# Stacked q and k of three attentions, read back per group of four heads in 8 KB runs

## What is computed

```python
x = x + attn_a(layernorm(x))    # 16 q heads, 4 kv heads of 16 channels, RoPE, causal by blocks of 128
x = x + moe(layernorm(x))       # 64 experts
x = x + attn_b(layernorm(x))    # 16 q heads, 4 kv heads, window of 128 and 4 sink tokens
x = x + moe(layernorm(x))
x = x + attn_c(layernorm(x))    # 16 q heads, 16 kv heads, RoPE, all tokens seen
x = x + ffn(layernorm(x))
x = x + latent_attn(layernorm(x))
x = x + ffn(layernorm(x))

# each of a, b, c, per head (d = 16):
scores = q @ k.T / 4            # 1024 x 1024, masked
y = softmax(scores) @ v
```

## Time and profile before

| | us |
|---|---|
| median of three runs | 2221.38 |
| profiled execution, its own time | 2218.32 |
| its span | 2216.3 |
| TensorE busy | 1916.7 (86%) |
| VectorE busy | 1164.1 (53%) |
| ScalarE busy | 912.3 (41%) |
| GpSimd busy | 597.5 (27%) |
| mean granted TensorE clock | 0.911 |

### The profile page before, as it was taken

How to read it: one execution, slowest core, us unless ns; L and a number is a source line. 1 busy time by engine, 2 the same in 40 slices (tenths; PEclk the granted TensorE clock), 3 DMA queues, 4 the chain that set the end, 5 groups by cost and what they waited for, 6 DMA issues and landing times. The chain is left out here.

```text
span 2216.3 us, 30788 instructions
## 1 busy us (share of the span) xinstructions
PE 1916.7 (86%) x10273; PEld 1241.9 (56%) x10273; DVE 1164.1 (53%) x2032; ACT 912.3 (41%) x1932; POOL 597.5 (27%) x488
## 2 busy tenths in 40 slices
PE   4499689999998498699999985499976899999997
PEld 3133467888885265587888863033344455555566
DVE  4476334444444354344444456488833467777743
ACT  1177433333333265333333332087751045555531
POOL 1000246656662100456656534000000011111100
PEclk8599789999999699799999997599997599999998
DMA  2700153444430700444444401900004000000000
GB/s 75 107 1 1 38 131 102 112 123 106 106 85 0 108 2 24 97 123 115 106 103 106 126 3 51 135 8 1 1 1 102 0 1 1 0 0 0 0 1 20
DMA packets 128262, 123.11 MB, mean 56 GB/s; under 512 B 81448, under 2 KB 108208, under 8 KB 128016
## 3 DMA queue, kind: packets, MB, share of 16 engines
q1 hardware_dynamic: 128176, 121.99, 24.5%
HBM read 113.30 MB, written 8.65 MB: 55 GB/s over the span
## 5 line engine op out<-in xcount | busy, mean ns | idle before, releaser
L667 DVE TENSOR_TENSOR e_inner_lo<-e_inner_b,e_inner_hi 128x512 fp32r<-128x512 f32 x192 | 251.5, 1310 | 391.6 <-ACT e_inner_hi L614 391.6
L647 POOL TENSOR_TENSOR e_wsilu<-e_silu_b,e_rw 128x512 f32<-128x512 f32 x192 | 262.0, 1365 | 212.0 <-ACT e_silu_b L621 158.6
L554 PE MATMUL psum<-e_x_hi,e_w_hi 128*128 128x512 f32 x768 | 305.6, 398 | 5.8 <-DVE e_inner_b L678 4.4
L554 PE MATMUL psum<-e_x_lo,e_w_hi 128*128 128x512 f32 x768 | 301.1, 392 | 0.0
L554 PE MATMUL psum<-e_x_hi,e_w_lo 128*128 128x512 f32 x768 | 301.0, 392 | 0.0
L621 ACT ACTIVATE e_silu_b<-psum 128x512 f32<-128x512 f32 x192 | 114.7, 597 | 365.2 <-PE psum L554 365.2
L655 POOL TENSOR_TENSOR e_w_lo<-e_w_raw,e_w_hi 128x384 fp32r<-128x384 f32 x180 | 215.4, 1197 | 134.2 <-ACT e_w_hi L608 112.8
L1202 DVE TENSOR_REDUCE c_mx<-psum 128x1 f32<-128x1024 f32 x128 | 151.4, 1220 | 63.4 <-PE psum L1079 63.4
L554 PEld LDWEIGHTS psum<-e_x_hi,e_w_hi 128*128 128x128 f32 x768 | 145.6, 190 | 48.3 <-DVE e_inner_b L678 18.3
L1650 ACT ACTIVATE la_probs<-psum,la_negmax 128x256 f32<-128x256 f32 (+7 forms) x128 | 96.2, 752 | 175.9 <-DVE la_negmax L1737 175.9
L554 PEld LDWEIGHTS psum<-e_x_hi,e_w_lo 128*128 128x128 f32 x768 | 145.5, 189 | 31.0
(11 more groups left out here) (303 smaller groups left out, 3116.9 us busy)
## 6 DMA issues: line engine op xcount, KB each, us to landing
e_rw<-e_rw_dram SPq DMA_DIRECT2D x64, 384.0 KB, 5.8
e_rw<-e_rw_dram SPq DMA_DIRECT2D x64, 256.0 KB, 5.4
e_w_raw<-in_L_ffn_w_gate SPq DMA_DIRECT2D x64, 192.0 KB, 2.6
e_w_raw<-in_L_ffn_w_up SPq DMA_DIRECT2D x64, 192.0 KB, 2.6
e_w_raw<-in_L_ffn_w_down SPq DMA_DIRECT2D x32, 384.0 KB, 3.5
e_rw<-e_rw_dram SPq DMA_DIRECT2D x64, 128.0 KB, 5.3
a_qs<-a_parts_dram SPq DMA_DIRECT2D x12, 256.0 KB, 9.3
b_qs<-b_parts_dram SPq DMA_DIRECT2D x12, 256.0 KB, 9.4
```

The lines of the kernel that those rows point to most:

```text
L554: last = nc.tensor.matmul(bank[u % 2][:], parts.up_or_gate(a, s, which, k, j), parts.x[b][:, k, h * HALF:(h + 1) * HALF], start=(n == 0), ...
L647: nc.gpsimd.tensor_tensor(wsilu[:, u % 2, :], silu[:, u % 2, :], rw[:, s, j, h * HALF:(h + 1) * HALF], ALU.mult).then_inc(weighted, 1)
L667: nc.vector.tensor_tensor(inner_parts[1][:, u % 3, :], inner[:, u % 2, :], inner_parts[0][:, u % 3, :], ALU.subtract).then_inc(low_made, 1)
```

## The change

Three things differ. First, the parts in DRAM are laid out as (chunk, part, channel, head, token), so that four heads of one channel are 8 KB in one piece. A unit's parts are stored by three DMAs, one per part, in place of one. Second, the reads: per group of four heads, q is read in three pieces of 48, 32 and 16 partitions, each repeating one part 3, 2 or 1 times (`broadcast_to`); k, where the group has keys of its own, in three pieces that take the parts in turn. `PAIRS` is put in the order that this needs. Third, one semaphore per group: TensorE waits for a group's stacks ahead of the first maximum of phases 0, 2, 4 and 6.

```diff
-PAIRS = [(0, 0), (0, 1), (1, 0), (0, 2), (1, 1), (2, 0)]
+PAIRS = [(0, 0), (0, 1), (0, 2), (1, 0), (1, 1), (2, 0)]
...
-        stacked = [core.sem(f"{tag}_stk{c}") for c in range(HEADS * HD // P)]
+        stacked = [core.sem(f"{tag}_stk{g}") for g in range(HEADS // QUART)]
...
+RUNS = [(0, 3), (3, 2), (5, 1)]
+
+
+def stacks_of_group(cfg, g):
+
+    return len(RUNS) * (2 if cfg.kv_heads == HEADS or g == 0 else 1)
...
-    parts_dram = nc.dram_tensor(f"{tag}_parts_dram", (PARTS, C, P, T), BF16, kind="Internal").ap()
+    parts_dram = nc.dram_tensor(f"{tag}_parts_dram", (C, PARTS, HD, P // HD, T), BF16, kind="Internal").ap()
...
-                sp.dma_start(parts_dram[:, j, 0:rows_of[j], h * HALF:(h + 1) * HALF].rearrange("a p t -> p a t"),
-                             part[0:rows_of[j], :, j, h * HALF:(h + 1) * HALF]).then_inc(parts_stored, 16)
+                for w in range(PARTS):
+                    sp.dma_start(parts_dram[j, w, :, 0:rows_of[j] // HD, h * HALF:(h + 1) * HALF].rearrange("d h t -> h d t"),
+                                 part[0:rows_of[j], w, j, h * HALF:(h + 1) * HALF]).then_inc(parts_stored, 16)
...
-                sp.wait_ge(parts_stored, 16 * (n + 1))
-                for g, (pq, pk) in enumerate(PAIRS):
-                    todo = [(qs, pq, c)]
-                    if c < cfg.k_chunks:
-                        todo.append((ks, pk, QC + c))
-                    for dst, which, i in todo:
-                        heads = rows_of[i] // HD
-                        h0 = 8 * c
-                        sp.dma_start(dst[g * HD:(g + 1) * HD, h0:h0 + heads, :],
-                                     parts_dram[which, i, 0:rows_of[i], :].rearrange("(h d) t -> d h t", d=HD)
-                                     ).then_inc(stacked[c], 16)
-
+                sp.wait_ge(parts_stored, 16 * PARTS * (n + 1))
+                for g in range(2 * c, 2 * c + 2):
+                    h0 = QUART * (g % 2)
+                    todo = [(qs, c, QUART * g, h0, QUART, False)]
+                    if cfg.kv_heads == HEADS or g == 0:
+                        todo.append((ks, QC + c, QUART * g, h0, QUART, True))
+                    for dst, i, to, frm, heads, in_turn in todo:
+                        for n0, (r0, reps) in enumerate(RUNS):
+                            rows = parts_dram[i, :, :, frm:frm + heads, :].rearrange("w d h t -> w d (h t)")
+                            if in_turn:
+                                some = rows[0:reps].rearrange("w d n -> (w d) n")
+                            else:
+                                some = rows[n0:n0 + 1].broadcast_to([reps, HD, heads * T])
+                            sp.dma_start(dst[r0 * HD:(r0 + reps) * HD, to:to + heads, :].rearrange("p h t -> p (h t)"), some).then_inc(stacked[g], 16)
...
-            pe.wait_ge(stacked[0], 16 * stacks_of_chunk(cfg, 0))
             for what, *args in order:
                 if what == "max":
-                    if args == [PHASES // 2, 0, 0]:
-                        pe.wait_ge(stacked[1], 16 * stacks_of_chunk(cfg, 1))
+                    if args[0] % 2 == 0 and args[1:] == [0, 0]:
+                        pe.wait_ge(stacked[args[0] // 2], 16 * stacks_of_group(cfg, args[0] // 2))
                     maxima(*args)
```

More of the change, by code:

```diff
@@ L763, in attention @@
         project_out(core, tag, ctxs, wo, wo_loaded, extra=core.xn if tag == "c" else None)
-def stacks_of_chunk(cfg, c):
-    return len(PAIRS) * (2 if c < cfg.k_chunks else 1)
+RUNS = [(0, 3), (3, 2), (5, 1)]
+def stacks_of_group(cfg, g):
+    return len(RUNS) * (2 if cfg.kv_heads == HEADS or g == 0 else 1)
 def project_and_stack(core, tag, cfg, norm, v, qs, ks, part, wo, stacked, wo_loaded):
```

## The result

| | before | after |
|---|---|---|
| median, us | 2221.16 (20 runs) | 2226.03 (20 runs) |
| profiled execution, its own time | 2218.32 | 2225.67 |
| its span | 2216.3 | 2223.6 |

A forecast was written before the change was run, and what follows sets the result against it. DMA transfers ahead of each attention's first maximum, 72.5 us in all, were taken as the bound. Stores +20.8, reads of group 0 -16.1 and added waits nothing gave +4.7 on 2218.3: 2223, as a median 2226; range 2190 to 2243.

The forecast's parts named there:

- Stores: First store issue to stores landed, in all three attentions: 8 or 4 engines make this +20.8 us (+7.6 to +34.0).
- term of 12.6 us for the four units: Stores in a: the four units ahead of the first reads take 12.6 us from first bytes at 55.7, landing at 68.7.
- Reads of group 0: First read issue to first maximum, in all three attentions: 18.8 us each (14.6 to 21.5), sum -16.1 (-28.8 to -8.0).
- 39 rows of 0.34 us are 13.3 us: Reads of group 0: engine 0 carries most, 33 rows of q and 6 of k, 8 KB each, in 13.3 us.
- Rates by partitions: Stores and reads: rate goes by partitions touched at a time, not bytes; 337 to 386 GB/s from 128, 185 from 64.
- Few engines for a short outermost dimension: New stores and q reads: only as many of the 16 engines work as the outermost dimension (8, 4, 3, 2) has entries.
- All engines, 2181 us: First rival, stores and reads: all 16 engines carry every piece, stores cost as before, about -40 us, 2181; chance 0.15.
- The added waits: TensorE's waits ahead of phases 2, 4 and 6 cost nothing; the tightest is b, with phase 2 due 21.6 us after first maximum.
- What would show it: Signs in the trace: stores about 14 us, reads about 19 in all three, high rate 3 us, then two or three engines.

The follow-up runs named there:

- e4: The kernel before with only the new DRAM layout and three stores a unit, its own twelve reads per chunk and two semaphores kept: 2233.90 us, ratio 1.0054.
- e5: The kernel before with three stores a unit, one per part, in place of one, its own layout and reads kept: 2223.68 us, ratio 1.0012.
- e8: The changed kernel with k pieces issued ahead of q pieces and the 48-row q piece cut into 32 and 16 rows: 2220.61 us, 0.9997 of the kernel before.
- e12: The changed kernel with group 1's reads, and all behind them, issued only when group 0 has landed: 2216.44 us, 0.9974 of the kernel before.
- e3: The changed kernel with the 48-row q piece cut into 32 and 16 rows: 2224.34 us, 1.0011 of the kernel before.
- e7: The changed kernel with a group's k pieces issued ahead of its q pieces, same DMAs: 2221.01 us, 1.0001 of the kernel before.
- e1: The changed kernel with a channel's repeats next to each other, so every read's outermost dimension is 16, stores untouched: 2193.84 us, 0.9880 of the kernel before.
- e6: e2 with k's reads of the first chunk issued on ScalarE's queue in another order of blocks: 2186.32 us, 0.9840 of the kernel before.
- e10: e2, one queue, with a group's twelve pieces ordered so that neighbours write different partitions and share no block: 2189.97 us, 0.9841 of the kernel before.
- e11: e9 with group 1's reads moved from the projection's block to the attention's: 2188.36 us, 0.9837 of the kernel before.
- e2: The kernel before with only its reads and waits made per group of four heads, own stores, layout and 2 KB runs: 2192.52 us, ratio 0.9877.
- e9: The kernel before with group semaphores, one-head reads into 48, 32 and 16 partitions, channels outermost, first chunk's k on ScalarE's queue: 2194.94 us, ratio 0.9872.

## Why the prediction was right, and where it was not

The total was right: +4.7 foretold, +4.9 between the medians, +7.3 in the profiled span. The mechanism was right too: few engines, in the stores and in the reads. The sizes of its two large terms were not, and that the total came out is in good part luck.

- **Stores**, taken as +20.8 (7.6 to 34.0), were +12.3. The mechanism (8 or 4 engines) is shown by the share of 0.51 and 0.27; that the stores alone cost this, by e4. Its term of 12.6 us for the four units was an estimate that let other engines slow each one for half of the time, and no run shows it: they ran at 21 to 23 GB/s each, and 11.0, 11.2 and 11.0 us less 0.9 ahead and 0.4 behind leave 9.7 to 9.9. Nor does one show the 17.0 us that its upper end comes from, 192 rows of 1 KB at 11.6 GB/s an engine: 11.6 was measured on 64 partitions with all 16 engines. What I had at nothing, three issues a unit in place of one, is 1.9, 1.7 and 0.3 us where all engines work (e5).
- **Reads of group 0**, taken as -16.1 (-28.8 to -8.0), were -4.4, outside their own bounds. The failed step is "39 rows of 0.34 us are 13.3 us", to which I added 1 us as all that the other transfers cost. It has the engines that carry q's rows nearly alone on the memory from the start. In fact the others don't wait for them: the share is 0.95 (167 GB/s from 69 to 75 us in a) although q's first two pieces can use three engines and two, so the rest have run ahead into k's pieces, group 1's and, in c, group 1's keys. This lasts some 7 us in a and b and 11 to 12 in c, and an engine then gets 11 to 12 GB/s (e8: 186 GB/s for all 16 in a, 175 in c). e12 confirms it: less behind, shorter reads. The rest of the 17.5 us behind its 18.8, 3.2 us for engines of the 48-row piece that slow each other, and the 5.9 in its upper end of 21.5 were estimates that no run shows: with that piece in two the reads are 0.1 to 1.7 us shorter (e3, e8 against e7). And the start is slower than the 0.9 us taken from before: in a the stretch from 66.8 to 67.8 has 25 GB/s at a share of 0.27, which is three rows of 8 KB at 1.4 us each, and the rest starts near 68.8, 3 us after the first issue.
- **Rates by partitions.** "Half of them, half the rate" fits the stores: half of the 386 GB/s of 128 partitions is 193, near the 185 of 64. It does not go on to the reads into 16 partitions, where an eighth of 386 would be 48 and 114 to 125 were measured. The share of 1.03 that the prediction gives as the least of the earlier trace rows isn't in them either; they have 0.59, then 1.08 to 1.10.
- The errors are of opposite sign, 8.5 and 11.7 us, and cancel but for 3. A reader should take the mechanism from this prediction and not its arithmetic.
- **Few engines for a short outermost dimension**: shown, by e1, which changes only the order of the dimensions, and with it which row of the stack a repeat goes to. With 2 or 3 copies in front the traces show a share of 0.12, two engines, in the last stretch shown of e8, and of 0.18, three, in the changed kernel's from 78 to 80; e1 has 1.02.
- **All engines, 2181 us** (first rival): it did not come, but e1 has the reads that it supposed. With these, 11.7, 11.6 and 11.9, and stores unchanged the sum would be -37, where the rival had -40; with three stores a unit on all engines, as in e5, it would be -33. These sums are estimates, no run has both.
- **The added waits** cost nothing: the trace has one wait of TensorE for a stack in each attention, that for group 0, and none for a later group.
- **What would show it**: stores of about 14 us were announced (11 measured), reads of about 19 in all three (22 to 24), a high rate for the first 3 us and then two or three engines (it was 7 us in a and b and 12 in c, then that).

The best versions are e6, e10 and e11, at 0.984 of the kernel before: 1.6% faster, and their intervals overlap, so none is shown to be the best. None keeps the 8 KB runs.

Open is why the first rows of a q piece on three engines take 1.4 us each. That c's reads in e7 and e8 stay at 22.4 and 22.3 fits the running ahead: in e8 all engines are busy from 1390 to 1401 (share 1.02, 175 GB/s), 11 us against 7 in a. It isn't shown, since keys first was not run with group 1 held back. Nor was a version run with 8 KB runs in the reads and stores on 16 engines, which is e1 without its slow stores.

## What to carry to other kernels

Look at the outermost dimension of both sides of every DMA before its size or the length of its runs: here a repeat or a head count of 2, 3, 4 or 8 in front left half of the engines or more idle (shares of 0.12, 0.18, 0.27 and 0.51), and putting the 16 channels in front cost a changed order of rows and nothing else, and took the reads from 21.9, 22.3 and 23.9 us to 11.7, 11.6 and 11.9 (e1). The end of these reads was set by the few engines that carry q's rows, and they moved 11 to 12 GB/s each while the others ran ahead, against 24.5 by themselves (e8); so order and withhold later transfers where a few engines carry the critical one. And against the kernel before, a finer wait, with half the bytes ahead of the first use, was worth some 29 us (e2), and changes to the transfers on top of it another 3 to 9 (e6, e10, e11, by medians and by ratios).

## What the runs showed of the hardware that I had not expected

- Two DMA engines by themselves keep 24.5 GB/s each on rows of 8 KB (e8: share 0.12, 49 GB/s); 16 at once on 48, 32 and 16 partitions get 182 (e1) to 186 GB/s (e8) together, 11.4 to 11.6 each.
- The engines of one queue don't keep step: those that a transfer leaves out go on to what stands behind it (a share of 0.95 from 69 to 75 us in the changed kernel's a), and slow the ones that carry it. Held back, that gave 1.1, 1.9 and 4.5 us of reads in a, b and c (e12).
- Three stores of 128 KB in place of one of 384 KB (for the k units of a and b 64 KB and 192), with all engines, end 1.7 to 1.9 us later in a and b after four units (e5).
- Reads into 16 partitions carry 119 GB/s from one queue (e2), 128 with neighbours on different partitions (e10), 163 from two queues that are at different blocks (e6), each over the same 8 us of a.
- A DMA issued ahead of a block's end delays what TensorE does behind it: with 24 issues in 14.15 us in e9, the first matmul of the next block started at 75.96, 0.5 us after the last issue, while e11, with half of them moved, had its first maximum 1.6 us sooner after the first read issue.
